# Clipped attention: value rows three rows behind the scores, and a ring of exponentials six rows long

## The chip, the core and the metric

The kernel runs on one core of a Trainium2 chip. The metric is the time of one execution on the device in microseconds, the median of several runs. Beside it there is one profiled execution, whose trace gives every instruction's start and length on the five engines: TensorE (PE, with its weight loads as PEld), VectorE (DVE), ScalarE (ACT), GpSimd (POOL), and SyncE (SP), which here only issues DMAs.

## The reference

Four stages are added to a residual x of shape (4, 1024, 128), each as x + layernorm(f(layernorm(x))):

1. a causal attention with 16 heads of 8, whose scores are clipped to -10 and 10 before the softmax, and an output projection;
2. a latent (low-rank key and value) attention with rotary parts, followed by a mixture of eight experts, two for each token, and a shared one;
3. a causal attention with 16 heads of 8 without the clip;
4. a low-rank feed-forward layer with gelu.

The change concerns the three attentions. For a head of the clipped one:

```
scores = clip(q @ k.T * 8 ** -0.5, -10, 10) + causal mask
out    = softmax(scores) @ v
```

## The kernel before

All in one launch, the kernel goes through phases with a barrier between them: projections for the clipped attention (a0), the attention, output projection and latent projections, the latent attention (am), its end, the experts, projections, the last attention (a1), and the end with the feed-forward layer. One function, `attention(name, scale, latent, clip)`, is the body of all three attentions.

An attention has 16 items: 4 batch elements times 4 groups of four heads (`QUAD`). Within an item, scores stand with keys on partitions and queries along the free axis. Their blocks of 128x128 below and on the diagonal, 36 per head, are packed into nine rows (`ROWS_P`) of 512 columns for each of the four heads. `S_UNITS` says which blocks a row holds: rows 0, 1, 2 and 7, 8 hold the blocks on the diagonal (`DIAG`). For each row g:

- TensorE makes the scores in PSUM (`score_unit`, L926). In the clipped and the latent attention a unit is two heads wide (1024 columns), so a row has two units and an item 18; three pairs of banks take turns (`NSB`), so that unit t waits until the exponential of unit t - 3 has been taken. In a1 a unit is one head wide.
- ScalarE takes the exponential of a unit from PSUM into a ring in SBUF (L1045). In the clipped attention no maximum is subtracted.
- VectorE clips the exponentials in place, to exp(-10) and exp(10) (L1217, clipped attention alone; in the others it makes row maxima for the item ahead, L1157).
- GpSimd sets the part above the diagonal in diagonal blocks to zero (L1110), 16 instructions to an item, in rows 7, 8, 0, 1 and 2: 2, 4, 2, 4 and 4 of them.
- TensorE multiplies the row with the values (`value_row`, L978) and sums in one of the output banks. `V_ROWS` says what a value row reads: value row 3 reads, beside row 3, two blocks of row 2. An output has two halves; value rows 0 to 2 (`A_ROWS` = 3) fill the first, 3 to 8 the second.

Each engine has its instructions in an order written out by hand and runs them in that order. TensorE's order is set by the lag `PLAG`: after the scores of row g it issues value row g - PLAG, and in the first rows of an item the last value rows of the item before:

```
for g in range(ROWS_P):
    ...
        score_unit(n, i, g, e)
    ...
    if g >= PLAG:
        value_row(n, i, g - PLAG)
    elif last != 0:
        value_row(n - 1, i - 1, g - PLAG + ROWS_P)
```

A value row waits for the clips of its row (`s_clip`; in the other attentions for the exponentials), for its selects (`s_sel`) and, where it begins a half, for the copy that has emptied the bank (`s_oc`). The copy of an output half from PSUM to `o_two` (L1198 on VectorE in the clipped attention, L1033 on ScalarE in the others) stands in its engine's order at rows PLAG and A_ROWS + PLAG; SyncE stores it from there.

The ring holds `PRING` = 4 rows of exponentials in `area` (the tile q_buf). Before the first exponential of a row, ScalarE waits until the value row that read the old contents is done:

```
act.wait_ge(s_pv, ROWS_P * n + g + 1 + (g - PRING == A_ROWS - 1) + BASE)
```

The added term is for the ring place of row 2, which value row 3 reads as well. The buffer `pr_buf` has 12 units of 512 columns; in the attentions its last four are `o_two` and its first eight lie idle.

In the last items of a0 and a1 other work is woven in: VectorE inverts three sums (L1205), SyncE spreads them, and GpSimd multiplies output rows with them (L677).

Of the kernel before, what the change touches and what calls it, by code (L numbers as in the profile page):

```python
# [32 lines left out]
HEADS, QUAD = 16, 4  # L33
NQ = HEADS // QUAD
ITEMS = BATCH * NQ
UNIT = CH
ROWS_P = (KB * (KB + 1) // 2) * P // UNIT
# [37 lines left out]
def build(nc, ins, consts, out):  # L75
    stack = ExitStack()
    with stack:
        def sb(name, shape, dt=F32):
            return stack.enter_context(nc.sbuf_tensor(name, shape, dt))
# [95 lines left out]
        pr_buf = sb("pr_buf", [P, 12, UNIT])  # L175
# [503 lines left out]
        def attention(name, scale, latent, clip):  # L679
# [7 lines left out]
            LEAD = 4  # L687
            V_ROWS_OUT = VW if latent else VS
            STORES = 1 if latent else QUAD + 1
            PLAG, PRING = 2, 4  # L690
            M_WIDE, M_BUFS = (1, 3) if latent else (2, 2)
            M_PAIRS = 2 * ROWS_P
            REDUCES = UNITS // M_WIDE
            assert NQ % PRING == 0
            o_bank, s_bank0, m_bank0 = 0, O_BUFS, O_BUFS + WIDE * NSB
            assert clip or m_bank0 + M_WIDE * M_BUFS == 8
            DIMS = MD
# [10 lines left out]
                qs, ks, vs = qs8, ks8, vs8  # L708
            block_max = o_sb[:, 0, 0:QUAD * KB * 4].rearrange("p (j s) -> p j s", j=QUAD)
            ring = area[:, 16384:24576].rearrange("p (u t) -> p u t", t=UNIT)  # L710

            def units(i, g, j, cnt=1):

                at = ((ROWS_P * i + g) % PRING) * QUAD + j
                return ring[:, at:at + cnt, :]

            def keys(rows, s, p, k):

# [71 lines left out]
            with nc.Block() as block:  # L790
# [124 lines left out]
                def _(pe):  # L915
# [47 lines left out]
                    def value_row(n, i, g):  # L963

                        s = slot(i)
                        if clip:
                            pe.wait_ge(s_clip, EXPS * n + EXPS_R * (g + 1) + BASE)
                        else:
                            pe.wait_ge(s_e, EXPS * n + EXPS_R * (g + 1) + NSB + BASE)
                        pe.wait_ge(s_sel, DIAGS * n + diags_before[g + 1] + BASE)  # L970
                        half = 0 if g < A_ROWS else 1
                        if g in (0, A_ROWS):
                            pe.wait_ge(s_oc, 2 * n + half + 1 + BASE)
                        for r, k, q0, nq, off in V_ROWS[g]:
                            lo = q0 - 4 * half
                            for j in range(QUAD):
                                v = vs[:, s, k, 0:VW] if latent else vs[:, s, k, j * VS:(j + 1) * VS]
                                mm = nc.tensor.matmul(  # L978
                                    ps[VW * j:VW * j + V_ROWS_OUT, o_bank + half % O_BUFS, lo * P:(lo + nq) * P], v,
                                    units(i, r, j)[:, 0, off * P:(off + nq) * P],  # L980
                                    start=(k == 0), stop=(g in (A_ROWS - 1, ROWS_P - 1)), tile_position=(0, VW * j),
                                    skip_group_check=True)
                        mm.then_inc(s_pv, 1)
# [43 lines left out]
                def _(act):  # L1027
# [8 lines left out]
                    def item(b, i, last):  # L1036
                        n = b * NQ + i
                        for g in range(ROWS_P):
                            for e in range(EXPS_R):
                                t = EXPS_R * g + e  # L1040
                                bank = s_bank0 + WIDE * (t % NSB)
                                act.wait_ge(s_s, EXPS * n + t + 1 + BASE)
                                if e == 0:
                                    act.wait_ge(s_pv, ROWS_P * n + g + 1 + (g - PRING == A_ROWS - 1) + BASE)
                                nc.scalar.activation(units(i, g, WIDE * e, WIDE), ps[:, bank:bank + WIDE, :],  # L1045
                                                     ACT.Exp, scale=scale).then_inc(s_e, 1)
                                if has_max and e == 0:
                                    if g == PLAG and last != 0:
                                        copy_output(b, i - 1, 1)
                                    if g == A_ROWS + PLAG:  # L1050
                                        copy_output(b, i, 0)
# [12 lines left out]
                def _(pool):  # L1064
# [33 lines left out]
                    def item(b, i, last):  # L1098
                        n = b * NQ + i
                        for g in range(ROWS_P):  # L1100
                            for p in range(2):
                                if g not in DIAG:
                                    continue
                                if clip:
                                    wait_alone(pool, s_clip, EXPS * n + EXPS_R * g + p + 1)
                                else:
                                    wait_alone(pool, s_e, EXPS * n + EXPS_R * g + EXPS_R * (p + 1) // 2 + NSB)
                                for off in DIAG[g]:
                                    blk = units(i, g, 2 * p, 2)[:, :, off * P:(off + 1) * P]
                                    nc.gpsimd.affine_select(out=blk, in_=blk, compare_op=ALU.is_ge, fill=0.0, base=0,  # L1110
                                                            pattern=[[0, 2], [1, P]], channel_multiplier=-1)\
                                        .then_inc(s_sel, 1)
                            if not latent and last == ITEMS - 1 and g == 2:
                                pool.wait_ge(s_rows, 16 * (EARLY + 8))
                                for c in range(4):
                                    multiply_rows(c)
                            if latent and g == 2 and (last is None or last + 2 < ITEMS):
                                cast(b, i, 2)
                            if has_max and not latent and g == ROWS_P - LEAD and (last is None or last + 1 < ITEMS):
                                split_maxima(n + 1, (i + 1) % 2)  # L1120
# [1076 lines left out]
        project_heads8("p0", w_sb["wq0"][:, :], w_sb["wk0"][:, :], w_sb["wv0"][:, :], True)  # L2197
        end_phase()
        attention("a0", 8.0 ** -0.5, latent=False, clip=True)
        end_phase()  # L2200
        prepare("am")
        finish_and_project_latent(w_sb["wout0"][:, :])
        end_phase()
        attention("am", 0.125, latent=True, clip=False)
        end_phase()
        finish_latent()
# [4 lines left out]
        project_heads8("p1", w_sb["wq1"][:, :], w_sb["wk1"][:, :], w_sb["wv1"][:, :], False)  # L2211
        end_phase()
        attention("a1", 8.0 ** -0.5, latent=False, clip=False)
        end_phase()
        finish_and_ffn()
# [86 lines left out]
```

## Time and profile before

| | |
|---|---|
| median of 3 runs | 1895.78 us (1890.99 to 1896.42) |
| span of the profiled execution | 1888.6 us |
| its own time | not given apart from the span |
| TensorE, ScalarE, VectorE, GpSimd busy, share of the span | 86%, 61%, 69%, 35% |
| mean granted clock of TensorE | 0.957 |
| clipped attention, about 60 to 365 us | 305 us |
| latent attention, about 522 to 1054 us | 532 us |
| last attention, about 1390 to 1790 us | 400 us |

The span runs from the first to the last instruction; the time of a run holds what lies around it too. Busy time is the time in which an engine had an instruction at work; the rows name the engine, the line of the kernel, and tiles with their shapes. `PEclk` is the clock granted to TensorE as a share of its full speed: 1.00 is 2.4 GHz and 0.50 is 1.2 GHz. `[0.76 <-PE ps L926]` says that the engine stood idle for 0.76 us before the instruction and what released it.

### The profile page before, as it was taken

What the parts mean: (1) busy time and instruction counts of PE and PEld (TensorE: products, weight loads), DVE (VectorE), ACT (ScalarE), POOL (GpSimd) and SP (SyncE); (2) the same over time, 40 slices, a digit from 0 to 9 for tenths busy, and PEclk for the clock granted to TensorE, in tenths of its full rate; (3) what the DMA queues carried; (4) which work ended last, traced back from release to release, by engine and by line L of the source; (5) the groups of instructions that cost most, each with busy time, mean ns of one, the idle gap of its engine ahead of it and who ended that gap; (6) DMA issues with size and microseconds to landing.
All of it is one profiled execution on the core that took longest, in us unless ns stands there. A gap on an engine that the chain in (4) does not pass through costs nothing. (4 is left out here: it accounts for less than half of the span.)

```text
span 1888.6 us, 36620 instructions
## 1 busy us (share of the span) xinstructions
PE 1615.3 (86%) x12310; PEld 685.0 (36%) x12310; DVE 1294.7 (69%) x2458; ACT 1142.9 (61%) x1788; POOL 661.0 (35%) x1223
## 2 busy tenths in 40 slices
PE   5778787597899999999999888987698888888787
PEld 3321212153343443434434554544333333333233
DVE  6678778576677677776773246565498888889164
ACT  7699999543055555555556434332537787787755
POOL 6465655676322232322322001112512322332373
PEclk9899999799999999999999999898899999999997
DMA  8632334257332221313210310000712222222201
GB/s 243 135 67 57 63 60 123 65 121 175 57 66 45 61 60 41 78 44 63 58 42 24 132 58 1 0 0 1 223 25 50 49 50 49 50 49 65 49 26 45
DMA packets 92080, 125.99 MB, mean 67 GB/s; under 512 B 24533, under 2 KB 64085, under 8 KB 91686
## 3 DMA queue, kind: packets, MB, share of 16 engines
q1 hardware_dynamic: 89814, 121.30, 28.0%
q10 hardware_dynamic: 2096, 2.47, 0.4%
q8 instruction: 101, 1.65, 0.4%
q14 instruction: 69, 0.57, 0.1%
HBM read 76.03 MB, written 47.58 MB: 65 GB/s over the span
## 5 line engine op out<-in xcount | busy, mean ns | idle before, releaser
L1045 ACT ACTIVATE q_buf<-ps 128x1024 f32<-128x1024 f32 (+1 forms) x1152 | 864.4, 821 | 399.5 <-PE ps L926 393.4
L1157 DVE TENSOR_REDUCE o_sb<-ps 128x1 f32<-128x512 f32 (+3 forms) x864 | 709.9, 865 | 197.5 <-PE ps L957 189.8
L1110 POOL TENSOR_SCALAR_AFFINE_SELECT q_buf<-q_buf 128x256 f32<-128x256 f32 x768 | 364.3, 499 | 728.1 <-ACT q_buf L1045 595.2
L978 PE MATMUL ps<-q_buf,v_buf 128*9 128x512 f32 (+7 forms) x4608 | 462.7, 497 | 59.5 <-POOL q_buf L1110 54.7
L926 PE MATMUL ps<-q_buf,k_buf 49*128 49x512 f32 (+3 forms) x1536 | 309.4, 502 | 0.0
L926 PE MATMUL ps<-q_buf 48*128 48x512 bf16 (+7 forms) x1536 | 260.0, 332 | 51.9 <-ACT q_buf L1045 44.1
L1217 DVE TENSOR_SCALAR q_buf<-q_buf 128x1024 f32<-128x1024 f32 x288 | 218.1, 766 | 56.9 <-ACT q_buf L1045 52.0
L978 PEld LDWEIGHTS ps<-q_buf,v_buf 128*9 128x9 f32 (+1 forms) x4608 | 95.2, 96 | 253.6 <-issue 139.3
L926 PEld LDWEIGHTS ps<-q_buf 48*128 48x128 bf16 (+1 forms) x1536 | 76.6, 94 | 304.7 <-ACT q_buf L1045 251.6
L926 PEld LDWEIGHTS ps<-q_buf,k_buf 49*128 49x128 f32 x1536 | 133.0, 186 | 118.9 <-ACT q_buf L1045 53.7
L957 PE MATMUL ps<-k_buf,q_buf 48*128 48x512 bf16 (+3 forms) x768 | 118.2, 324 | 11.4 <-DVE o_sb L1157 7.8
L957 PE MATMUL ps<-q_buf 48*128 48x512 bf16 (+3 forms) x768 | 126.8, 325 | 0.7
L951 PE MATMUL ps<-causal_k,causal_q 64*128 64x128 bf16 x1024 | 110.2, 217 | 11.8 <-DVE o_sb L1157 5.9
L447 PE MATMUL ps<-w_wg,identity 128*128 128x512 f32 (+1 forms) x214 | 92.5, 550 | 30.9 <-PEq L112 30.9
L951 PEld LDWEIGHTS ps<-causal_k,causal_q 64*128 64x128 bf16 x1024 | 55.7, 94 | 92.3 <-DVE o_sb L1157 84.7
L316 DVE BATCH_NORM_STATS2 q_buf<-ps 128x6 f32<-128x128 f32 x96 | 21.4, 286 | 81.7 <-PE ps L2038 56.0
L364 ACT ACTIVATE q_buf<-ps,q_buf 128x128 f32<-128x128 f32 x96 | 36.2, 461 | 62.4 <-POOL q_buf L348 62.4
L957 PEld LDWEIGHTS ps<-k_buf,q_buf 48*128 48x128 bf16 x768 | 41.8, 94 | 74.0 <-DVE o_sb L1157 46.3
L452 PE MATMUL ps<-identity,q_buf 128*128 128x128 f32 x160 | 27.8, 301 | 44.5 <-ACT q_buf L364 36.7
L447 PEld LDWEIGHTS ps<-w_wg,identity 128*128 128x128 f32 x214 | 38.1, 202 | 69.2 <-issue 68.7
L1779 ACT ACTIVATE q_buf<-ps 128x512 f32<-128x512 f32 (+1 forms) x40 | 23.9, 596 | 54.6 <-PE ps L1850 54.6
L957 PEld LDWEIGHTS ps<-q_buf 48*128 48x128 bf16 x768 | 48.4, 94 | 18.5 <-DVE o_sb L1157 4.5
(179 smaller groups left out, 1575.2 us busy)
## 6 DMA issues: line engine op xcount, KB each, us to landing
q_buf<-qm_d SPq DMA_DIRECT2D x32, 384.0 KB, 6.9
qm_d<-pr_buf SPq DMA_DIRECT2D x80, 128.0 KB, 2.4
o_d<-pr_buf SPq DMA_DIRECT2D x16, 512.0 KB, 2.7
q_buf<-o_d SPq DMA_DIRECT2D x8, 1024.0 KB, 5.1
q_d<-q_buf SPq DMA_DIRECT2D x48, 128.0 KB, 2.1
k_d<-q_buf SPq DMA_DIRECT2D x48, 128.0 KB, 1.9
k_buf<-km_d SPq DMA_DIRECT2D x32, 192.0 KB, 6.9
q_buf<-q_d SPq DMA_DIRECT2D x60, 96.0 KB
```

The lines of the kernel that those rows point to most:

```text
L364: i = nc.scalar.activation(dst[:, t, :], src[:, t, :], ACT.Identity, scale=self.rstd[:, r, t:t + 1], bias=self.minus_m[:, r, t:t + 1])
L447: nc.tensor.matmul(ps[:, bank, 0:columns], identity[:, :], w_sb["wg"][:, 0:columns], start=True, stop=True)
L452: i = nc.tensor.transpose(ps[:, bank, t * P:(t + 1) * P], src[:, t, :], identity[:, :])
L926: mm = nc.tensor.matmul(ps[:, bank + w, off * P:(off + nq) * P], keys(rows, s, p, k), qs[rows, s, p, q0 * P:(q0 + nq) * P], start=True, st ...
L951: nc.tensor.matmul(ps[:, bank[pr], (o_ + nk - 1) * P:(o_ + nk) * P], causal_q[rows, :], causal_k[rows, :], start=True, stop=False, skip_gr ...
L957: mm = nc.tensor.matmul(ps[:, bank[pr], o_ * P:(o_ + nk) * P], (qm if latent else qs)[rows, s, p, q * P:(q + 1) * P], km[rows, s, kk] if l ...
L978: mm = nc.tensor.matmul(ps[VW * j:VW * j + V_ROWS_OUT, o_bank + half % O_BUFS, lo * P:(lo + nq) * P], v, units(i, r, j)[:, 0, off * P:(off ...
L1045: nc.scalar.activation(units(i, g, WIDE * e, WIDE), ps[:, bank:bank + WIDE, :], ACT.Exp, scale=scale).then_inc(s_e, 1)
L1110: nc.gpsimd.affine_select(out=blk, in_=blk, compare_op=ALU.is_ge, fill=0.0, base=0, pattern=[[0, 2], [1, P]], channel_multiplier=-1)\
L1157: nc.vector.tensor_reduce(to, sc, AX_X, ALU.max).then_inc(s_mr, 1)
L1217: nc.vector.tensor_scalar(two, two, float(np.exp(-10.0)), float(np.exp(10.0)), ALU.max, ALU.min).then_inc(s_clip, 1)
L1779: nc.scalar.activation(silu[0:rows, (GP * u + j) % 2, :], ps[0:rows, 2 + (GP * u + j) % 2, :], ACT.Silu).then_inc(s_si, 1)
```

## The change

The lag of the value rows is three in the clipped attention and stays two in the others. The ring of exponentials is six rows long in all three attentions: the first four places are where they were, the last two are the first eight units of `pr_buf`. The waits for the ring and the rows at which outputs are copied follow from `PLAG` and `PRING`.

```diff
@@ -687,11 +687,11 @@
             LEAD = 4
             V_ROWS_OUT = VW if latent else VS
             STORES = 1 if latent else QUAD + 1
-            PLAG, PRING = 2, 4
+            PLAG, PRING = (3 if clip else 2), 6
             M_WIDE, M_BUFS = (1, 3) if latent else (2, 2)
             M_PAIRS = 2 * ROWS_P
             REDUCES = UNITS // M_WIDE
-            assert NQ % PRING == 0
+            assert NQ * ROWS_P % PRING == 0
             o_bank, s_bank0, m_bank0 = 0, O_BUFS, O_BUFS + WIDE * NSB
             assert clip or m_bank0 + M_WIDE * M_BUFS == 8
             DIMS = MD
@@ -708,11 +708,15 @@
                 qs, ks, vs = qs8, ks8, vs8
             block_max = o_sb[:, 0, 0:QUAD * KB * 4].rearrange("p (j s) -> p j s", j=QUAD)
             ring = area[:, 16384:24576].rearrange("p (u t) -> p u t", t=UNIT)
+            RING_ROWS = 4
 
             def units(i, g, j, cnt=1):
 
-                at = ((ROWS_P * i + g) % PRING) * QUAD + j
-                return ring[:, at:at + cnt, :]
+                row = (ROWS_P * i + g) % PRING
+                if row < RING_ROWS:
+                    return ring[:, row * QUAD + j:row * QUAD + j + cnt, :]
+                at = (row - RING_ROWS) * QUAD + j
+                return pr_buf[:, at:at + cnt, :]
 
             def keys(rows, s, p, k):
 
```

## Rows read from the trace of the kernel before

**Rows 1.** The page: busy time of the engines over the span.

```profile
PE 1615.3 (86%) x12310; PEld 685.0 (36%) x12310; DVE 1294.7 (69%) x2458; ACT 1142.9 (61%) x1788; POOL 661.0 (35%) x1223
```

**Rows 2.** Busy time by stretch: selects, one item, clipped attention, latent attention.

```profile
core 0: us, PE busy (x) PEld busy (x) DVE busy (x) ACT busy (x) POOL busy (x), PEclk, DMA share, GB/s
242.71:252.78 10.07, 6.68 (x74) 2.02 (x74) 8.34 (x12) 9.31 (x11) 10.07 (x15) 1.00 0.62 98
235.97:253.91 17.94, 14.28 (x146) 3.63 (x144) 14.53 (x21) 16.81 (x18) 10.48 (x16) 1.00 0.37 61
60.00:365.00 305.00, 239.47 (x2311) 60.82 (x2312) 238.10 (x324) 269.52 (x288) 174.09 (x264) 0.95 0.38 73
522.00:1054.00 532.00, 516.66 (x4242) 215.75 (x4246) 348.67 (x617) 305.64 (x319) 139.43 (x284) 1.00 0.24 51
```

**Rows 3.** Groups of instructions in the clipped attention, 60 to 365 us.

```profile
L1045 ACT ACTIVATE q_buf<-ps 128x1024 f32<-128x1024 f32 x288 | 269.5, 1050 | 33.5 <-PE ps L926 33.2
L1217 DVE TENSOR_SCALAR q_buf<-q_buf 128x1024 f32<-128x1024 f32 x288 | 218.1, 766 | 56.9 <-ACT q_buf L1045 52.0
```

**Rows 4.** Waits of ScalarE: clipped, latent and last attention (total, times, longest).

```profile
ACT q_buf L1045 <- PE ps L926: 33.2, 36, 11.1
...
ACT q_buf L1045 <- PE ps L926: 248.7, 176, 31.3
...
ACT q_buf L1045 <- PE ps L926: 111.4, 140, 33.2
```

**Rows 5.** ScalarE in order of time, clipped attention: start, us, instruction [wait before].

```profile
61.26 5.61 ACT L1045 ACTIVATE q_buf<-ps 128x1024 f32<-128x1024 f32 x6 [11.05 <-PE ps L926]
67.69 1.94 ACT L1045 ACTIVATE q_buf<-ps 128x1024 f32<-128x1024 f32 x2 [0.82 <-PE ps L926]
70.18 12.94 ACT L1045 ACTIVATE q_buf<-ps 128x1024 f32<-128x1024 f32 x14 [0.55 <-PE ps L926]
...
102.89 5.71 ACT L1045 ACTIVATE q_buf<-ps 128x1024 f32<-128x1024 f32 x6 [1.82 <-PE ps L926]
...
235.97 11.22 ACT L1045 ACTIVATE q_buf<-ps 128x1024 f32<-128x1024 f32 x12 [0.36 <-PE ps L926]
247.94 5.61 ACT L1045 ACTIVATE q_buf<-ps 128x1024 f32<-128x1024 f32 x6 [0.76 <-PE ps L926]
...
351.26 1.94 ACT L1045 ACTIVATE q_buf<-ps 128x1024 f32<-128x1024 f32 x2 [0.23 <-PE ps L926]
```

**Rows 6.** All engines in order of time, items 9 and 10.

```profile
241.62 0.41 POOL L1110 TENSOR_SCALAR_AFFINE_SELECT q_buf<-q_buf 128x256 f32<-128x256 f32 x1 [6.79 <-DVE q_buf L1217]
...
242.71 10.07 POOL L1110 TENSOR_SCALAR_AFFINE_SELECT q_buf<-q_buf 128x256 f32<-128x256 f32 x15 [0.68 <-DVE q_buf L1217]
...
246.53 1.05 PE L978 MATMUL ps<-q_buf,v_buf 128*9 128x384 f32 x16 [1.20 <-POOL q_buf L1110]
...
247.51 0.61 PE L926 MATMUL ps<-q_buf 48*128 48x256 bf16 x8
...
249.00 0.69 DVE L1217 TENSOR_SCALAR q_buf<-q_buf 128x1024 f32<-128x1024 f32 x1 [0.84 <-ACT q_buf L1045]
...
252.93 0.62 PE L978 MATMUL ps<-q_buf,v_buf 128*9 128x256 f32 x8 [1.23 <-POOL q_buf L1110]
```

**Rows 7.** TensorE in order of time at the low clock; the start by stretch.

```profile
65.21 1.90 PE L978 MATMUL ps<-q_buf,v_buf 128*9 128x512 f32 x8 [0.34 <-DVE q_buf L1217]
...
68.04 1.77 PE L978 MATMUL ps<-q_buf,v_buf 128*9 128x384 f32 x16
...
100.41 1.89 PE L978 MATMUL ps<-q_buf,v_buf 128*9 128x384 f32 x16 [1.20 <-POOL q_buf L1110]
...
60.00:69.00 9.00, 7.08 (x40) 1.70 (x44) 5.94 (x8) 6.92 (x8) 5.17 (x10) 0.50 0.70 111
```

**Rows 8.** All engines in order of time, last item.

```profile
344.15 6.78 POOL L677 TENSOR_TENSOR q_buf<-q_buf 128x512 f32<-128x512 f32 x4
...
348.64 6.27 DVE L1217 TENSOR_SCALAR q_buf<-q_buf 128x1024 f32<-128x1024 f32 x7
```

## The prediction

> **What bounds the kernel now.** I read the page first. Over the whole span no engine is full: TensorE shows 86%, ScalarE 61% [rows 1]. Such shares average stages with different limits, so the second view is the table of stretches, one for each attention [rows 2]. The latent attention is TensorE's: 516.66 us busy in 532. The clipped attention is another matter: in its 305 us ScalarE works 269.52 us, more than TensorE and VectorE, which stand level at 239 and 238.
>
> The groups of that stretch [rows 3] say what ScalarE does: 288 exponentials of 128x1024 and nothing else. In a run without a wait 12 of them take 11.22 us [rows 5], so one takes 0.935 us, and an item (one batch element and four heads, 18 exponentials) costs ScalarE at least 18 x 0.935 = 16.83 us. The table gives an item as 17.94 us from run to run [rows 2]. The third view, the waits of ScalarE, says where the rest is: 33.2 us before the exponentials, all of it for score matmuls (L926), and 11.1 of it is the wait ahead of the first one, which is no part of the loop [rows 4]. 22.1 us are left, and they are what a better order inside this stage could win.
>
> The fourth view, ScalarE in order of time, shows the pattern: a run of 12, a wait of 0.36, a run of 6, a wait of 0.76, in nearly every item [rows 5]. Counting 18 to an item from the first one, the run at 235.97 begins with exponential 10 (row 5) of item 9, and the one at 247.94 with exponential 4 (row 2) of item 10. So the scores of rows 2 and 5 are late. The fifth view, all engines through that item, says why [rows 6]. TensorE works in order, and ahead of the scores of row 2 stands value row 8 of the item before, ahead of those of row 5 value row 2. Both waited for GpSimd (1.20 and 1.23 us). GpSimd blanks the diagonal blocks: 16 selects per item, all in rows 7, 8, 0, 1 and 2, one of 0.41 us and then 15 in one piece of 10.07 us. These five rows last 5 x 1.87 = 9.35 us on ScalarE, so GpSimd falls behind through them, and each value row inherits the delay.
>
> This can be checked by numbers. Value row 8 starts at 246.53, the scores behind it 0.98 later, the exponential 0.43 after those. ScalarE was done with exponential 3 at 235.97 + 12 x 0.935 = 247.19. To cost nothing the value row had to start by 247.19 - 1.41 = 245.78, and it is 0.75 late: the wait of 0.76. Value row 2, with two blocks only, starts at 252.93. ScalarE ran out at 247.94 + 5.61 = 253.55 and went on after the usual 0.36 [rows 5] at 253.91, which is 0.98 after the value row's start; so the latest start was 252.57.
>
> **The lag of three rows.** Nothing is added or removed: the same matmuls, exponentials, clips, selects and DMAs. On TensorE every value row of the clipped attention moves behind the scores of one more row, and VectorE's two copies of the output (0.68 us each) move with it from rows 2 and 5 to rows 3 and 6. So the scores that stand behind a value row are needed two exponentials, 1.87 us, later, while GpSimd is ready as before. Put into an item without gaps:
>
> - Value row 8 has to start by 245.78 + 1.87 = 247.65; its selects let it go at 246.53. Margin 1.12 us, the wait of 0.76 is gone.
> - Value row 2: exponential 11 of item 10 is the 20th after 235.97 to end without a gap, at 254.67 after 235.97 + 20 x 0.935; less 0.98 is 253.69. Its selects let it go at 252.93. Margin 0.76 us, so the wait of 0.36 is gone too. This is the tightest place.
> - Value rows 7, 0 and 1 lie between these two in GpSimd's piece of 15 and stand behind fewer selects than row 2; they get the same 1.87 us. I price them at nothing, since the rows between show no wait of ScalarE.
>
> What the moved work passes: the copies stand in VectorE's queue after the first clip of their row and wait for value rows 8 and 2, which in the new order are done before that clip is (value row 2 by 252.93 + 0.62 = 253.55, the first clip of row 6 about 256.3); behind them stand only clips. The stores on SyncE's queue follow the copies one row later, and the buffer that they empty is asked for again two items later. VectorE's load per item is 18 clips and two copies, 14.53 us busy [rows 2], under 16.83.
>
> **The ring of six rows.** In the clipped attention it is what the lag needs: value row 3 reads the exponentials of row 2 again, it now stands behind the scores of row 6, and in a ring of four row 6 would want the place of row 2 before. With six places every place is free before the scores of its new row are done, so no wait comes in. In the two other attentions the lag stays two, and there a place of the ring of four was already free by the order of TensorE's queue: the value row that frees it stands ahead of the scores that the exponential waits for anyway. Their waits of ScalarE are 248.7 and 111.4 us, all for scores and none for a value row [rows 4]. So I price the ring there at 0. From both sides: a gain would need a wait for a value row, and there is none; a loss would need slower writes into the other buffer, for which ScalarE has 248.7 and 111.4 us of room in these two. In the clipped attention it has none: there a third of the exponentials goes to the new buffer, and 1% on them would be 96 x 0.009 = 0.9 us. I take 0 for both (bounds 0 and 0.9).
>
> **The sum.** Of the 22.1 us these remain:
>
> - The start. TensorE's clock is at 0.50, its level of 1.2 GHz, up to 69 us [rows 7], and there two waits of 0.82 and 0.55 stand ahead of rows 3 and 4 [rows 5]. With value row 0 moved behind the scores of row 3, most of the slow stretch holds scores alone. I leave 0.3 (bounds 0 and 1.4).
> - Drops of the clock. At 100.41 a value row took 1.89 us for the usual 1.05, and the wait behind it was 1.82 for 0.76: 1.06 more [rows 5, 7]. Of the 35 waits in the order of time three places are like this. With margins of 0.76 and more most of it is absorbed; I leave 0.3 each, 1.0 (bounds 0 and 3.2). Ahead of this one TensorE had waited 1.20 us for selects, a wait that goes, so the drop may go with it.
> - The last item. GpSimd multiplies four output rows there in 6.78 us, VectorE's clips beside it go at 6.27 / 7 = 0.90, and the last one ends at 354.91 while the last exponential ends at 353.20 [rows 5, 8]. VectorE sets the end there, so the last gaps won by ScalarE are partly lost: 0.5 (bounds 0 and 1.1, an item's gaps).
>
> 22.1 - 0.3 - 1.0 - 0.5 = 20.3 us. The span goes from 1888.6 to 1868.3. The median of the runs, 1895.78, lies 7.2 above the span, and I let that stand: 1875.5 us. The bounds alone give gains of 22.1 and 22.1 - (1.4 + 3.2 + 1.1 + 0.9) = 15.5 us, 1873.7 to 1880.3.
>
> **Rivals.**
>
> *GpSimd takes part of it back.* A select takes 0.41 us by itself and 0.67 in the piece of 15, a clip 0.69 by itself [rows 6] and 0.766 on average [rows 3], so they disturb each other, and the gaps that vanish make the clips denser. The margin of value row 2 is 0.76 us over 15 selects, 0.05 each, 8% of 0.67. Denser clips alone (10.8 in 10.07 us where there were about 10) add some 0.3 us, which the margin holds. Were each select 0.1 us slower, value row 2 would be 1.5 - 0.76 = 0.74 late in each item, and 16 x 0.74 = 12 us of the gain would go: 1887.5. Halfway, 1881.5. Chance 0.11.
>
> *The two engines shut each other out, no change.* If each select waited out a whole clip, it would take 0.41 + 0.69 = 1.10, GpSimd would need 16 x 1.10 = 17.6 us per item, and the period could fall from 17.94 to 17.6 only: 16 x 0.34 = 5 us, 1890.5, at the edge of no change. Against it: in the 10.07 us of the piece, 15 selects and about 10.5 clips went through (12 instructions of VectorE are counted there, one a copy, the outer ones cut [rows 2]), which one after the other are 15 x 0.41 + 10.5 x 0.69 = 13.4 us. So they do overlap, even where GpSimd has no pause. Full exclusion would also make an item 18 x 0.69 + 16 x 0.41 = 18.98 us, above the measured 17.94; if it set in with denser clips, the stage would be 16 x 1.04 = 17 us slower, 1912. Chance 0.03 for no change and 0.01 for slower. (The Trainium skill, SBUF — State Buffer, section Who interferes with whom, has this as its single rule: VectorE in a 2-port mode, which tensor_scalar can enter, and GpSimd exclude each other for a whole instruction. By it the item would be 18.98 and the change worth nothing; the piece of 10.07 us speaks against it in that strict form.)
>
> *TensorE's clock, the other sign.* At the low level a row costs TensorE 68.04 - 65.21 = 2.83 us from one value row to the next in the first item, against ScalarE's 1.87, so each such row costs 0.96 us. If the new order brought TensorE's clock down more often, 27 rows at the low level, 76 us of this stage, would eat the gain and 5.7 us more. From there it is slower; 40 rows would give 1875.5 + 38 = 1913.5. Now it is low in 9 us at the start and in three short drops. Against it: the wait of TensorE ahead of the drop shown [rows 7] goes away, and the mean work of TensorE per time rises as the stage shrinks. Chance 0.03.
>
> **How the numbers follow.** The forecast has 0.82, its own range is 1871 to 1882 with the scatter of the runs (1890.99 to 1896.42). The first rival reaches to 1887.5, so the range of eight in ten is 1869 to 1886. A measurement of this kernel can tell about 0.3%, 5.7 us. Faster by more: 0.82 and nearly all of the first rival, 0.92. Within: 0.04. Slower: 0.04.
>
> **What the profile after would show.** The period of an item in ScalarE's order of time at 16.8 to 16.9 us; its waits after the first exponential at 1 to 4 us in all; the waits for GpSimd before value rows 7 and 8 gone and the one before row 2 short; the piece of 15 selects at 10.1 to 10.5 us; the latent and last attention as long as before. The forecast is wrong if that piece is over 10.9 us, or if ScalarE's waits come back in other rows with VectorE's clips as the late ones.

## The result, and the profile after

The median of four runs is 1877.88 us (1877.59 to 1880.88) against 1895.47 for the kernel before in four: a ratio of 0.9913, with an interval of 0.9894 to 0.9933. That is 17.6 us faster; forecast were 20.3 and a time of 1875.5, range 1869 to 1886. Run once more beside other kernels it gave 1876.81 against 1892.38, 0.9923 (0.9898 to 0.9947), 15.6 us. Each ratio is an estimate from single executions, so it need not be the quotient of the two medians. Two executions far above their kernels' others, 2941.38 us (the kernel before, among 29) and 5066.31 us (the lag alone, among 10), are in the medians below and not in the ratios.

Busy time by stretch, the changed kernel, with the columns of [rows 2]: the piece of 15 selects in one item, an item, and the clipped attention.

```profile
180.86:191.92 11.06, 8.78 (x88) 2.27 (x86) 9.96 (x14) 11.06 (x13) 11.06 (x15) 1.00 0.57 93
175.94:193.06 17.12, 14.68 (x146) 3.59 (x144) 14.75 (x21) 16.72 (x19) 11.48 (x16) 1.00 0.38 65
60.00:348.00 288.00, 242.85 (x2312) 60.20 (x2312) 241.13 (x327) 267.29 (x288) 190.40 (x264) 0.96 0.41 78
```

An item takes 17.12 us where it took 17.94 [rows 2]; forecast was 16.83. Its selects take 11.06 us where the same 15 took 10.07. TensorE's granted clock is full in both stretches.

ScalarE in order of time, the changed kernel. The exponentials now go to two tiles, so runs end at a change of tile too; a run without a bracket began without a wait.

```profile
60.99 7.44 ACT L1049 ACTIVATE q_buf<-ps 128x1024 f32<-128x1024 f32 x8 [11.49 <-PE ps L930]
68.84 1.94 ACT L1049 ACTIVATE pr_buf<-ps 128x1024 f32<-128x1024 f32 x2 [0.41 <-PE ps L930]
71.64 1.94 ACT L1049 ACTIVATE pr_buf<-ps 128x1024 f32<-128x1024 f32 x2 [0.85 <-PE ps L930]
...
175.94 7.55 ACT L1049 ACTIVATE q_buf<-ps 128x1024 f32<-128x1024 f32 x8 [0.40 <-PE ps L930]
183.33 3.83 ACT L1049 ACTIVATE pr_buf<-ps 128x1024 f32<-128x1024 f32 x4
186.94 5.71 ACT L1049 ACTIVATE q_buf<-ps 128x1024 f32<-128x1024 f32 x6
193.06 1.94 ACT L1049 ACTIVATE q_buf<-ps 128x1024 f32<-128x1024 f32 x2 [0.40 <-PE ps L930]
...
329.95 1.94 ACT L1049 ACTIVATE q_buf<-ps 128x1024 f32<-128x1024 f32 x2 [1.04 <-PE ps L930]
332.69 3.77 ACT L1049 ACTIVATE pr_buf<-ps 128x1024 f32<-128x1024 f32 x4 [0.81 <-PE ps L930]
```

Where two waits stood in an item [rows 5], one is left, of 0.36 to 0.40 us, 18 exponentials after the one before it. Counted from the first exponential it stands ahead of exponential 12, row 6, and so behind value row 2. The last item has two long ones. From the first exponential to the end of the last the loop takes 332.69 + 3.77 - 60.99 = 275.5 us against 351.26 + 1.94 - 61.26 = 291.9 [rows 5], 16.5 less.

Waits of ScalarE in the clipped attention, the changed kernel (total, times, longest):

```profile
ACT q_buf L1049 <- PE ps L930: 17.5, 15, 11.5
ACT pr_buf L1049 <- PE ps L930: 2.1, 3, 0.9
```

17.5 + 2.1 - 11.5 = 8.1 us of waits are left of 22.1 [rows 4]; forecast were 1.8.

All engines in order of time through the same item, the changed kernel:

```profile
179.77 0.41 POOL L1114 TENSOR_SCALAR_AFFINE_SELECT q_buf<-q_buf 128x256 f32<-128x256 f32 x1 [4.96 <-DVE q_buf L1221]
...
180.86 5.46 POOL L1114 TENSOR_SCALAR_AFFINE_SELECT q_buf<-q_buf 128x256 f32<-128x256 f32 x7 [0.68 <-DVE q_buf L1221]
...
184.88 1.05 PE L982 MATMUL ps<-q_buf,v_buf 128*9 128x384 f32 x16
...
186.27 5.66 POOL L1114 TENSOR_SCALAR_AFFINE_SELECT pr_buf<-pr_buf 128x256 f32<-128x256 f32 x8
...
189.25 1.05 PE L982 MATMUL ps<-pr_buf,v_buf 128*9 128x384 f32 x16 [0.64 <-POOL pr_buf L1114]
...
192.07 0.62 PE L982 MATMUL ps<-pr_buf,v_buf 128*9 128x256 f32 x8 [1.23 <-POOL pr_buf L1114]
```

Value row 8 (184.88) no longer waits for its selects; before it waited 1.20 us [rows 6]. Value row 1 (189.25) waits 0.64 us and costs ScalarE 0.1. Value row 2 (192.07) waits 1.23 us, as much as before, and ScalarE shows 0.40 us of wait behind it. The 16 selects of this item end 12.15 us after the first of them began (179.77 to 191.92); before it was 11.16 (241.62 to 252.78 [rows 6]).

The two traces differ by 12.6 us in span, less than by the loop's 16.5. From the end of the clipped loop on, the clock of TensorE falls at other places in them, and that gives 3.9 us back; the first and the last experiments below deal with it.

### The profile page after: what moved, and what is told of

The parts are those of the page before. It is cut to its first block and busy times, and to the rows that moved or that the text cites. A ratio compares the mean times of both kernels' runs of the same rounds, so it can differ in the third digit from the quotient of the medians.

```text
span 1876.0 us, 36620 instructions
## 1 busy us (share of the span) xinstructions
PE 1626.4 (87%) x12310; PEld 688.3 (37%) x12310; DVE 1297.0 (69%) x2458; ACT 1140.4 (61%) x1788; POOL 677.6 (36%) x1223
## 5 line engine op out<-in xcount | busy, mean ns | idle before, releaser
L1049 ACT ACTIVATE q_buf<-ps 128x1024 f32<-128x1024 f32 (+1 forms) x768 | 577.4, 832 | 288.3 <-PE ps L930 284.1
L1114 POOL TENSOR_SCALAR_AFFINE_SELECT q_buf<-q_buf 128x256 f32<-128x256 f32 x432 | 215.0, 520 | 407.3 <-ACT q_buf L1049 347.7
L1049 ACT ACTIVATE pr_buf<-ps 128x1024 f32<-128x1024 f32 (+1 forms) x384 | 291.4, 832 | 102.3 <-PE ps L930 100.6
L982 PE MATMUL ps<-q_buf,v_buf 128*9 128x512 f32 (+7 forms) x2880 | 307.3, 517 | 14.7 <-POOL q_buf L1114 11.9
L1114 POOL TENSOR_SCALAR_AFFINE_SELECT pr_buf<-pr_buf 128x256 f32<-128x256 f32 x336 | 166.3, 520 | 292.8 <-ACT pr_buf L1049 252.4
L982 PE MATMUL ps<-pr_buf,v_buf 128*9 128x512 f32 (+7 forms) x1728 | 157.4, 456 | 17.2 <-POOL pr_buf L1114 17.2
L1221 DVE TENSOR_SCALAR q_buf<-q_buf 128x1024 f32<-128x1024 f32 x192 | 147.2, 776 | 25.2 <-ACT q_buf L1049 21.6
L955 PE MATMUL ps<-causal_k,causal_q 64*128 64x128 bf16 x1024 | 110.8, 219 | 10.5 <-DVE o_sb L1161 4.7
L982 PEld LDWEIGHTS ps<-q_buf,v_buf 128*9 128x9 f32 (+1 forms) x2880 | 56.3, 95 | 125.1 <-issue 86.1
L1221 DVE TENSOR_SCALAR pr_buf<-pr_buf 128x1024 f32<-128x1024 f32 x96 | 73.9, 778 | 12.2 <-ACT pr_buf L1049 10.5
L982 PEld LDWEIGHTS ps<-pr_buf,v_buf 128*9 128x9 f32 (+1 forms) x1728 | 37.4, 96 | 94.0 <-issue 58.7
```

Of the source, the lines that this page charges most:

```text
L955: nc.tensor.matmul(ps[:, bank[pr], (o_ + nk - 1) * P:(o_ + nk) * P], causal_q[rows, :], causal_k[rows, :], start=True, stop=False, skip_gr ...
L982: mm = nc.tensor.matmul(ps[VW * j:VW * j + V_ROWS_OUT, o_bank + half % O_BUFS, lo * P:(lo + nq) * P], v, units(i, r, j)[:, 0, off * P:(off ...
L1221: nc.vector.tensor_scalar(two, two, float(np.exp(-10.0)), float(np.exp(10.0)), ALU.max, ALU.min).then_inc(s_clip, 1)
```

## Experiments

Twelve more runs follow. "The loop" is the time from the first start of the 288 exponentials of the clipped attention to their last start, taken from each trace (before 290.9, after 274.4 us). "The period" is the time from one item's first exponential to the next item's, in regular items.

### The kernel before, once more

No edit.

> The kernel before, unchanged. In the two traces the clipped loop is 16.5 us shorter after the change (290.9 to 274.4 us from the first to the last exponential), the span only 12.6, the median 17.6. Theory 1 (clock lottery in the latent attention's start): in the trace of after TensorE's clock is low for 17 us there and the stage is 5.2 us longer; in the one trace of before it is not. Then this second trace of the unchanged kernel shows, if its time is near 1895, that low stretch and a latent attention about 5 us longer than in the first. Theory 2 (the ring of six rows slows the latent attention): then this trace has the short latent attention, like the first, at 1895 us too.

Measured: 1897.22 us against 1893.05 for other runs of the same kernel, 1.0015 (0.9985 to 1.0046). Twelve runs of this one program spread from 1885.53 to 1912.28, and the time follows the mean granted clock of TensorE: 0.960 in the fastest, 0.937 in the slowest. The trace is that of the slowest. Its busy time by stretch, loop, then up to the latent loop, the latent loop, and up to the last attention:

```profile
61.00:353.00 292.00, 234.09 (x2280) 58.05 (x2276) 234.90 (x321) 268.98 (x288) 169.23 (x255) 0.97 0.39 76
353.00:532.00 179.00, 142.40 (x514) 68.18 (x512) 108.82 (x248) 46.51 (x100) 89.50 (x125) 0.80 0.49 108
532.00:1061.00 529.00, 513.90 (x4218) 214.69 (x4218) 347.34 (x614) 304.92 (x319) 138.06 (x282) 1.00 0.22 49
1061.00:1422.00 361.00, 297.80 (x1321) 175.43 (x1313) 199.85 (x554) 120.91 (x291) 57.54 (x91) 0.84 0.18 56
```

The clipped loop is 291.1 us, the latent one 528.5 (527.8 in the first trace), but the parts between them are 179.3 and 361.4 us for 171.5 and 343.8, at clocks of 0.80 and 0.84 for 0.88 and 0.91. So in these two traces the difference is made in the projections and the experts, and the loops can be compared between single traces. Both theories had this trace near 1895 us; it was a slower one. It does show the low stretch of the first theory, 13.6 us that end 1.5 us into the latent attention's exponentials. The latent item is 33.7 us in it, in the first trace and in after alike, so the second theory, a latent attention slowed by the ring, has nothing to stand on.

### The ring alone

```diff
-            PLAG, PRING = 2, 4
+            PLAG, PRING = 2, 6
```

with the new `units`, against the kernel before.

> The ring of six rows alone, lag of two everywhere. Theory 1 (the ring does nothing by itself): the time of the kernel before within 0.2%, item period of the clipped attention 17.94 us. Theory 2 (slower writes or reads in the second buffer, or in the latent attention): slower by 1 to 5 us.

Measured: 1894.01 against 1893.05, 0.9995 (0.9965 to 1.0026). Loop 290.9 us, item period 17.94, latent item 33.7, item of the last attention 24.49 as before. The ring is worth nothing by itself, and costs nothing.

### The lag alone

```diff
-            PLAG, PRING = 2, 4
+            PLAG, PRING = (3 if clip else 2), 4
```

> The lag of three rows in the clipped attention with the ring of four. Theory: the exponential of row 6 now has to wait for value row 3, which stands behind the scores of row 6 and takes 1.48 us. ScalarE waits some 1 to 1.8 us for TensorE's value row once per item, item period 17.8 to 18.5 us, so the time is that of the kernel before within 0.5%. Rival (the ring is not needed, since value row 3 is done in time): period 17.1 us, time that of after, about 1878.

Measured: 1898.93 against 1893.05, 1.0022 (0.9992 to 1.0051); loop 297.7 us, 6.8 longer than before. ScalarE in order of time:

```profile
149.81 16.61 ACT L1045 ACTIVATE q_buf<-ps 128x1024 f32<-128x1024 f32 x18 [2.06 <-PE ps L978]
168.48 16.61 ACT L1045 ACTIVATE q_buf<-ps 128x1024 f32<-128x1024 f32 x18 [2.06 <-PE ps L978]
```

One wait of 2.06 us per item is left, and it is for a value row (L978), no longer for scores: exponential 12, the first of row 6, waits until value row 3 has read row 2's place. The period is 18.67 us, a little above the expected 17.8 to 18.5. The 18 exponentials between two waits run through in 16.61 us. So the lag needs the ring, and the two together do what neither does.

GpSimd in order of time, the same kernel:

```profile
154.60 11.03 POOL L1110 TENSOR_SCALAR_AFFINE_SELECT q_buf<-q_buf 128x256 f32<-128x256 f32 x15 [0.68 <-DVE q_buf L1217]
```

The 15 selects take 11.03 us here, as in after, although all of them work in q_buf; with the ring alone, where some of them work in pr_buf, they take 10.07. So the second buffer does not make them slower. The lag does: it takes the two waits of ScalarE out of the time of these selects, so more clips fall into it.

### The lag of four

```diff
-            PLAG, PRING = (3 if clip else 2), 6
+            PLAG, PRING = (4 if clip else 2), 6
```

> The lag of four rows in the clipped attention, ring of six. In after the only wait left in a regular item is one of 0.40 us ahead of row 6, behind value row 2, whose selects end too late. Theory (selects too slow by 0.4 us for a lag of three): with one more row the wait goes, item period 16.68 us (18 starts at 0.927), the clipped loop 7 us shorter, time about 1871. Rival (GpSimd or VectorE is the bound now): the period stays at 17.1 and the time at 1878.

Measured: 1871.5 against 1893.05, 0.9878 (0.9838 to 0.9917). The loop is 263.9 us, 10.5 less than after where 7 were expected, the period 16.50 for 16.68. Waits of ScalarE in the loop, kernel with a lag of four:

```profile
ACT q_buf L1049 <- PE ps L930: 12.1, 2, 11.6
ACT pr_buf L1049 <- PE ps L930: 0.4, 1, 0.4
```

12.1 + 0.4 - 11.6 = 0.9 us of recorded waits is left in the whole loop. ScalarE in order of time, the same kernel:

```profile
150.32 7.86 ACT L1049 ACTIVATE q_buf<-ps 128x1024 f32<-128x1024 f32 x8
157.55 4.29 ACT L1049 ACTIVATE pr_buf<-ps 128x1024 f32<-128x1024 f32 x4
```

Eight exponentials start within 157.55 - 150.32 = 7.23 us, so one takes 0.904, not the 0.935 that I had from a run's length over its count. Such a length holds the end of the last record, which reaches past the start that would follow, and starts a little late that get no bracket. The floor of an item is 18 x 0.904 = 16.27, and GpSimd and VectorE keep up with 16.50. Nearly all of the 0.23 us between the two lies in one step of each item, of 1.11 us from exponential 15 to 16; what it waits for was not tested. The theory holds, and its rival falls: neither engine was the bound in after, its selects only came too late.

### Selects of 8 columns

```diff
-    blk = units(i, g, 2 * p, 2)[:, :, off * P:(off + 1) * P]
+    blk = units(i, g, 2 * p, 2)[:, :, off * P:off * P + (8 if clip else P)]
...
-                            pattern=[[0, 2], [1, P]], channel_multiplier=-1)\
+                            pattern=[[0, 2], [1, 8 if clip else P]], channel_multiplier=-1)\
```

in the kernel before (lag two, ring four) and in the changed one.

> The kernel before (lag two, ring four) with GpSimd's selects in the clipped attention 8 columns wide instead of 128: it leaves out blanking most of the diagonal blocks, all else is kept. Theory (the late value rows come from GpSimd's selects alone): TensorE no longer waits for GpSimd ahead of value rows 8 and 2, the item period falls from 17.94 to about 16.5 us as with a lag of four, the loop from 290.9 to about 264 us. Rival (the chain of exponential, clip and value row is itself too long for a lag of two): the period stays above 17.1.

> The changed kernel with the same selects of 8 columns; the same part is left out. Theory: period about 16.4 to 16.5 us, equal to the one with a lag of two and small selects within 0.1, so the lag is worth nothing once GpSimd is quick. Rival: the lag helps by itself, period lower by 0.3 or more than with a lag of two.

Measured, one run each: 1865.45 and 1866.72 us, beside 1890.81 for the kernel before. The loops are 268.3 and 263.2 us, the period 16.50 in both, a select 0.35 and 0.38 us on average. ScalarE in order of time, lag of two:

```profile
69.76 232.94 ACT L1045 ACTIVATE q_buf<-ps 128x1024 f32<-128x1024 f32 x254 [0.76 <-PE ps L926]
302.92 20.54 ACT L1045 ACTIVATE q_buf<-ps 128x1024 f32<-128x1024 f32 x22 [0.22 <-PE ps L926]
324.46 1.94 ACT L1045 ACTIVATE q_buf<-ps 128x1024 f32<-128x1024 f32 x2 [1.00 <-PE ps L926]
328.41 1.94 ACT L1045 ACTIVATE q_buf<-ps 128x1024 f32<-128x1024 f32 x2 [2.01 <-PE ps L926]
```

254 exponentials without a recorded wait: the selects made the waits of a regular item, and with quick ones a lag of two is long enough. One part of the theory did not come true: TensorE still waits for GpSimd in the kernel with a lag of two, 16.8 us in 40 waits between 80 and 310 us, in a regular item 0.4 us ahead of value rows 8, 1 and 2. The period of 16.50 us leaves them a cost of at most 0.23 us per item. The 5.1 us between the two loops lie at the start and in the last item, where the multiplications of GpSimd stand and the lag of three still helps.

### Half clips

```diff
-    two = units(i, g, 2 * p, 2)
+    two = units(i, g, 2 * p, 2)[:, :, 0:UNIT // 2]
```

in the changed kernel and in the kernel before; selects whole.

> The changed kernel with clips 512 columns wide instead of 1024 in two-head units (256 of each head's 512): it leaves out half of the clipping, the selects are whole. In after a select takes 0.40 us or, beside a clip, 0.85; 12 of 16 are slow. Theory (a select beside a clip waits for the clip): slow selects get shorter, below 0.65 us, the piece of 15 falls from 11.05 us to under 9.5, the wait ahead of row 6 goes, the period is about 16.5 us. Rival (selects are slow for another reason, the exponentials' writes or the matmuls' reads, or the piece is long by its own work): the piece stays above 10.5 us and the period at 17.1.

> The kernel before (lag two, ring four) with clips half as wide (half of the clipping is left out), selects whole. With a lag of three this took the slow selects from 0.85 to 0.6 us, the piece of 15 from 11.1 to 8.4. Theory (the time in which selects wait for clips is what makes the lag of two too short): the piece is under 8.6 us here too, and value row 2 and 8 come in time or nearly so: period 16.4 to 16.8 us. Rival (with a lag of two even quick selects are late): period above 17.1.

Measured, one run each: 1875.68 us with a lag of three and 1862.1 with two; the loops 263.2 and 264.8 us, the period 16.50 in both. (The difference of the two times is from outside the loop: in the first, the part between the latent and the last loop takes 362.2 us, with TensorE at the low clock for 116 of them, in the second 342.1 with 61.5.) GpSimd in order of time, lag of two with half clips:

```profile
176.68 0.41 POOL L1110 TENSOR_SCALAR_AFFINE_SELECT q_buf<-q_buf 128x256 f32<-128x256 f32 x1 [0.51 <-DVE q_buf L1217]
177.59 0.76 POOL L1110 TENSOR_SCALAR_AFFINE_SELECT q_buf<-q_buf 128x256 f32<-128x256 f32 x2 [0.51 <-DVE q_buf L1217]
178.77 1.30 POOL L1110 TENSOR_SCALAR_AFFINE_SELECT q_buf<-q_buf 128x256 f32<-128x256 f32 x3 [0.41 <-DVE q_buf L1217]
180.48 0.41 POOL L1110 TENSOR_SCALAR_AFFINE_SELECT q_buf<-q_buf 128x256 f32<-128x256 f32 x1 [0.41 <-DVE q_buf L1217]
181.30 3.77 POOL L1110 TENSOR_SCALAR_AFFINE_SELECT q_buf<-q_buf 128x256 f32<-128x256 f32 x8 [0.41 <-DVE q_buf L1217]
```

The selects are the same work as ever, and the 15 of an item are done in 181.30 + 3.77 - 176.68 = 8.39 us with pauses in which GpSimd waits for VectorE, for 10.07 without a pause before. The clips are shorter too, 0.47 us on average for 0.77, but that does not start the selects earlier: the first of an item begins 1.93 us after the first exponential of row 7, in before 1.89. The last ends 11.23 us after it, for 13.05. No select is above 0.7 us; with whole clips each is either 0.40 or 0.85 (up to 0.96). ScalarE, same kernel:

```profile
69.65 255.17 ACT L1045 ACTIVATE q_buf<-ps 128x1024 f32<-128x1024 f32 x278 [0.35 <-PE ps L926]
```

278 exponentials without a recorded wait, with a lag of two and a ring of four. So what made the lag of two too short is the time in which selects and clips hold each other up. Both theories on the clips hold; the rivals fall.

### The filler in the latent attention's start

```diff
                             for g in range(ROWS_P):
                                 for p in range(2):
                                     max_pair(0, 0, 0, 0, g, p)
                                     fill(s_bank0, 1, CH // 2)
+                            if latent:
+                                fill(s_bank0, 1)
                             for g in range(LEAD):
```

with a lag of four (twice) and of three.

> Lag of four, ring of six, and in the start of the latent attention one more filler matmul of 512 columns, where TensorE waits 0.97 us for VectorE between the maxima of item 0 and item 1. In after the clock falls to its low level at that wait (495.5 us) for 17 us, in the first trace of before it does not. Theory (the wait brings the drop): no low clock between the start of the latent attention's maxima and its loop, the time 3 to 5 us below the lag of four without the filler, some 1867. Rival (the drop comes and goes from run to run for other reasons): the same time as the lag of four, 1871, within the scatter.

> Lag of four and the filler, once more: clipped loop 263.6 us, 10.8 under after, no low stretch ahead of the latent loop; time 13 to 16 us under after and 26 to 31 under the kernel before. Rival: the loop's gain is lost elsewhere and the time is no more than 8 under after.

> The changed kernel with the one filler matmul in the start of the latent attention. If the 0.97 us wait brings the drop, the low stretch of 17 us between the maxima and the latent loop is missing and the time is 3 to 5 us under that of after. If it comes by chance, the time is that of after.

Measured: with a lag of four 1866.84 against 1890.81, 0.9868 (0.9831 to 0.9905), and 1865.17 against 1892.38, 0.9848 (0.9812 to 0.9883); with a lag of three 1873.57 against 1892.38, 0.9902 (0.9867 to 0.9936), beside 1876.81 for after. The loops are 263.6, 263.5 and 272.6 us. The stretch ahead of the latent loop, in after and in the first kernel with the filler:

```profile
493.00:510.00 17.00, 15.72 (x52) 6.01 (x54) 11.71 (x24) 0.30 (x1) 0.00 (x0) 0.57 0.43 80
```

```profile
480.00:499.00 19.00, 15.35 (x86) 6.81 (x86) 17.39 (x32) 0.03 (x1) 0.00 (x0) 1.00 0.31 57
```

TensorE in order of time in after, at the fall of the clock:

```profile
493.63 0.70 PE L447 MATMUL ps<-w_wg,identity 128*128 128x256 f32 x2
495.30 0.60 PE L961 MATMUL ps<-k_buf,q_buf 48*128 48x512 bf16 x2 [0.97 <-DVE o_sb L1161]
495.83 1.22 PE L447 MATMUL ps<-w_wg,identity 128*128 128x256 f32 x2
```

The clock falls right at the wait of 0.97 us, and the same filler that took 0.70 takes 1.22. The wait is in all eleven traces without the filler, 0.97 us in each, and in none of the three with it. Of the eleven, seven show the low stretch of 14 to 17 us and four do not, the first trace of before and the second of after among these; of the three none does. So the wait alone does not decide it. Where the stretch stands, the first exponential of the latent loop comes 13.8 to 14.4 us after the wait, and 10.4 where it does not: 3.4 to 4.0 us is what it costs. The three traces with the filler speak for the theory and are no proof: three traces without the stretch in a row would come by chance in (4/11)^3, one case in 20. The times fit 3 to 5 us (1866.84 for 1871.5 with a lag of four, 1873.57 for 1876.81 with three), but that is within the scatter. The second run with a lag of four came 11.6 us under after, where 13 to 16 were expected, and 27.2 under the kernel before, within the 26 to 31.

### The changed kernel, once more

No edit to the changed kernel.

> The changed kernel once more, beside the three below on one chip. The clipped loop is 274.4 us from the first to the last exponential, as in the first trace of after (it has been 290.9 to 291.1 in three traces with a lag of two), whatever the clock does elsewhere. The time about 16 us under the kernel before. Rival: the loop is another one, and the gain of 17.6 was partly scatter.

Measured: 1876.81 against 1892.38; loop 272.6 us, 1.8 less than in the first trace. Regular items are alike (17.07 to 17.12); the first trace has 2.11 and 1.83 us from one exponential to the next in the last item, this one 1.47 and 1.02, with TensorE's clock high there. The gain is no scatter: with a lag of two and whole work the loop is 290.9, 291.1 and 290.9 us (before twice, and the ring alone), in the changed order 274.4, 272.6 and 272.6 (after twice, and with the filler).

## Why the prediction was right, and where it was off

**The bound and the place.** Right. ScalarE was the bound of the clipped attention, its waits came from value rows 8 and 2, and these from the selects: with selects of 8 columns they vanish with a lag of two, but for those at the start and in the last items.

**The price of an exponential.** Off. I took 0.935 us from a run's length; the starts are 0.904 apart, as the lag of four shows. So an item costs ScalarE 16.27 us at least, a wait costs more than its bracket says (the 0.76 stands for 1.88 us between two starts instead of 0.90), and there was more to win than 22.1 us: 287 steps of 0.904 are 259.4 us, 31.5 less than the loop of before. The lag of four shortened the loop by 27.0 and the one of three by 16.5, with a forecast of 20.3.

**The margins.** Those of value rows 8, 7 and 0 held, and that of value row 1 but for 0.1 us. That of value row 2 did not. This is the step that failed: denser clips alone were to "add some 0.3 us, which the margin holds". The 15 selects took 11.06 us instead of 10.07, 0.99 more, above the margin of 0.76, and a wait of 0.36 to 0.40 us came back in 13 items: 5.0 of the 8.1 us left. The mechanism had been named as the first rival, with a chance of 0.11, and its price per select was 0.99 / 15 = 0.066 us, above the 0.05 of the margin and below the 0.1 of the rival. I had spread the cost of a clip over all selects. The records show it in steps: a select takes 0.40 us or 0.85. In one item of the trace of before, 10 of the 16 are slow, in one of after 12, and 2 x 0.45 is the 0.9 us.

The margin was also smaller than 0.76 us, for it had been worked out with 0.935 us per exponential. Counted from the start of the first exponential of row 7 (239.74 in before, 177.88 in after; the first select follows 1.9 us later in both), exponential 12 of the next item is due after 16 x 0.904 = 14.46 us, and value row 2 has to start 0.98 before that, at 13.48. In before it started at 252.93 - 239.74 = 13.19: a margin of 0.29 us, which the 0.3 of the forecast would have used up. In after it started at 192.07 - 177.88 = 14.19, 0.71 late, and that is how late the exponential came.

The prediction had named a piece of 15 selects over 10.9 us as a sign that its forecast is wrong, and the sign is there. Two more of its marks were missed: the period is 17.12 us for 16.8 to 16.9, the waits are 8.1 us for 1 to 4. The waits for GpSimd ahead of value rows 7 and 8 are gone, as it said.

**The two engines shut each other out.** The strict form stays refuted: in after, an item of 17.12 us holds 18 clips and 16 selects, which one after the other are 18.98. With a lag of four it is 16.50. A weaker form is right. With clips of half the width the slow selects fall from 0.85 to 0.6, so a select waits for a part of the clip beside it. (The Trainium skill, SBUF — State Buffer, section Who interferes with whom, has VectorE in a 2-port mode and GpSimd exclude each other for a whole instruction. The half clips show that the two do hold each other up. That one shuts the other out for its full recorded length does not fit 16.50 us for an item that would need 18.98.)

**The ring.** Right: 0 by itself, in all three attentions (the item takes as long as before in each, the time is the same within 0.3%), and needed by the lag: with the ring of four the wait is 2.06 us per item and the loop 6.8 us longer than before.

**The remains.** At the start 0.41 + 0.85 = 1.26 us stayed, not 0.3. The three drops of the clock in regular items are gone in both traces of after, where I had left 1.0; in the first trace one of 3.4 us lies in the last item instead. Each of the three had followed a wait of TensorE of 1.20 or 1.23 us for selects, ahead of value row 8 or 2. Such waits stand in nearly every item, though, and the clock fell at three of them; that fewer waits kept it up is plausible and was not tested apart. The last item kept 1.04 + 0.81 = 1.85 us in the first trace, not 0.5.

**From the span to the time.** The 7.2 us between span and median were no constant. In after a run took 1877.7 and its span was 1876.0, 1.7 us less. The span of before plus 1.7 is 1890.3, near the lowest of its four times, 1890.99, and 5 us under their median: the trace was of a run with the clock high where it often is not. So the forecast of the time came out nearer than its parts. The span was to be 1868.3 and was 1876.0, 7.7 us more; what lies between span and median was to be 7.2 and was 1.9, 5.3 less. That these two errors left only 2.4 us is luck.

## What to carry to other kernels

Where an engine runs full, take the price of an instruction from start to start, not from the length of a run over its count. A lag bought from margins has to be priced with the other engines as dense as they will be after it: here a margin put at 0.76 us, and 0.29 by the right price, met 0.99 us of new contention. If a lag is cheap, try one step more: four rows instead of three took 10.5 us more off the loop, and with the filler made the fastest version with its whole work, 1865.17 us. And where a long chain of waits goes back to two engines that hold each other up, look for a way to remove the cause, which may do nearly as much as a longer lag: with half of the clipping left out, as a test, a lag of two came within 0.9 us of the loop with a lag of four.

## What was not expected of the hardware

GpSimd's select of 128x256 takes 0.40 us or, beside a VectorE clip of 128x1024, 0.85, with little between; beside clips of half that width it is 0.6. The clip itself goes from 0.69 to as much as 0.96 in regular items.

The time of one program varied by 26.7 us from run to run (1885.53 to 1912.28), with the mean granted clock of TensorE from 0.960 to 0.937, and in the two traces of it, 22.0 us apart, nearly all of the difference lies outside the three attention loops.
